# Attention and experts on one core: the pair's shared tile in two column groups, eight places for weights, other orders at passage and end

## The reference

```python
Q, K, V = ste_sign(x * sign(bv_q)), ste_sign(x * sign(bv_k)), x * sign(bv_v)
attn = where(causal, sigmoid(einsum('btd,bsd->bts', Q, K) * d**-0.5 * 4.0), 0.0)
x = layernorm(x + einsum('bts,bsd->btd', attn, V))
probs = softmax(x @ w_router); top1 = argmax(probs); gate = probs[top1]
pos = place of the token among those of its expert; accepted = pos < 320
g, u = rows @ w_gate[e], rows @ w_up[e]              # rows: accepted tokens of expert e
y = (silu(g) * u) @ w_down[e]                        # w_gate, w_up, w_down: 256 x 256
x = layernorm(x + where(accepted, y * gate, 0))
```

## Time and profile before

| | |
|---|---|
| median of 3 runs | 561.88 us (561.63 to 563.4) |
| the profiled execution | 564.1 us |
| its span, first to last instruction | 562.3 us |
| PE busy | 526.3 us (94%) |
| DVE busy | 409.3 us (73%) |
| ACT busy | 375.4 us (67%) |
| POOL busy | 371.1 us (66%) |
| mean granted clock of TensorE | 0.987 of full speed |
| moved by DMA | 81.53 MB |

### The profile page before, as it was taken

One profiled execution on the slowest core, in us unless ns is written; L12 is line 12 of the kernel. 1 busy time (PEld: TensorE's weight loads), 2 busy tenths in 40 slices (PEclk: granted clock), 3 DMA queues, 4 the chain that ended last, 5 costly groups with the idle time before them and its releaser, 6 DMA issues.

```text
span 562.3 us, 12210 instructions
## 1 busy us (share of the span) xinstructions
PE 526.3 (94%) x4024; PEld 475.7 (85%) x4062; DVE 409.3 (73%) x1029; ACT 375.4 (67%) x743; POOL 371.1 (66%) x496
## 2 busy tenths in 40 slices
PE   6999999999999999999999889999999999999970
PEld 5889898898978988888989359999989999998960
DVE  4785868867878857779586447888878887878860
ACT  5886968859677787677784215666666667667641
POOL 4647878687777768696772631676757667676672
PEclk9999999999999999999999999999999999999995
DMA  7994233243322532313910063676767677766410
GB/s 253 372 354 145 76 95 79 91 133 98 116 70 77 164 95 99 71 38 45 325 54 22 21 170 86 190 206 203 209 188 217 196 211 204 224 180 216 143 37 25
DMA packets 91902, 81.53 MB, mean 145 GB/s; under 512 B 31626, under 2 KB 83066, under 8 KB 91840
## 3 DMA queue, kind: packets, MB, share of 16 engines
q1 hardware_dynamic: 84848, 66.39, 40.6%
q0 software_dynamic: 6912, 14.30, 7.1%
q10 hardware_dynamic: 80, 0.07, 0.0%
HBM read 44.33 MB, written 37.90 MB: 146 GB/s over the span
## 4 chain that ended last, share of the span: by engine, by line
PE 69%; DVE 9%; issue 8%; DMA 5%; POOL 2%; ACT 2%; SPq 2%; another core or an unknown queue 1%; DVEq 0%; POOLq 0%; ACTq 0%
PE ps L884 11%; PE ps L885 10%; PE ps L886 10%; PE ps L860 9%; PE ps L1035 5%; PE ps L1043 4%; PE ps L1036 4%; PE ps L1061 4%; DMA xall<-in_L_ffn_w_down_dram 3%; PE ps L903 2%; PE ps L1013 2%; PE ps L1058 1%; DVE hl_ring L1127 1%; PE ps L916 1%; POOL out_dram L593 1%
## 5 line engine op out<-in xcount | busy, mean ns | idle before, releaser
L884 PE MATMUL ps<-v_hl,hl_ring 128*128 128x256 f32 x544 | 176.1, 324 | 0.5 <-DVE hl_ring L1127 0.3
L885 PE MATMUL ps<-v_hl,hl_ring 128*128 128x256 f32 x544 | 153.4, 282 | 0.0
L886 PE MATMUL ps<-v_hl,hl_ring 128*128 128x256 f32 x544 | 153.1, 281 | 0.0
L593 POOL DMA_INDIRECT out_dram<-alone,ids x80 | 97.0, 1213 | 37.6 <-issue 32.5
L884 PEld LDWEIGHTS ps<-v_hl,hl_ring 128*128 128x128 f32 x544 | 103.3, 190 | 15.7 <-issue 1.1
L1127 DVE TENSOR_TENSOR hl_ring<-ps,hl_ring 128x512 fp32r<-128x512 f32 (+3 forms) x160 | 93.2, 600 | 18.6 <-ACT ps L669 14.3
L885 PEld LDWEIGHTS ps<-v_hl,hl_ring 128*128 128x128 f32 x544 | 103.6, 190 | 2.4
L886 PEld LDWEIGHTS ps<-v_hl,hl_ring 128*128 128x128 f32 x544 | 103.2, 190 | 0.0
L667 ACT ACTIVATE hl_ring<-ps 128x512 fp32r<-128x512 f32 (+3 forms) x160 | 85.9, 537 | 25.2 <-PE ps L863 10.4
L669 ACT ACTIVATE ps<-ps 128x512 f32<-128x512 f32 (+3 forms) x160 | 87.0, 544 | 0.0
L1035 PE MATMUL ps<-hl_ring,v_hl 128*128 128x320 f32 x256 | 82.5, 334 | 2.0 <-DVE act_r L1341 1.5
(11 more groups left out here) (154 smaller groups left out, 1091.8 us busy)
## 6 DMA issues: line engine op xcount, KB each, us to landing
expert_rows<-xs SPq DMA_DIRECT2D x40, 258.0 KB, 5.3
xs<-expert_rows SPq DMA_DIRECT2D x32, 258.0 KB, 2.8
xall<-in_L_attn_x_dram SPq DMA_DIRECT2D x16, 512.0 KB, 4.8
out_dram<-alone SPq DMA_DIRECT2D x16, 512.0 KB
xall<-in_L_ffn_w_gate_dram SPq DMA_DIRECT2D x32, 256.0 KB
xall<-in_L_ffn_w_up_dram SPq DMA_DIRECT2D x32, 256.0 KB
xall<-in_L_ffn_w_down_dram SPq DMA_DIRECT2D x32, 256.0 KB
xs<-expert_rows SPq DMA_DIRECT2D x31, 64.5 KB
```

The source lines that it names most:

```text
L593: g_.indirect_dma_start(out=out_rows, out_offset=bass.IndirectOffsetOnAxis(ap=ids[:, e % NIDS, t:t + 1], axis=0), in_=o_s[:, p, t, :], in_ ...
L884: mm(o, ah, v_hl[:, 0, j, :], start=(j == 0 and i % 2 == 0), stop=False, skip_group_check=True)
L885: mm(o, ah, v_hl[:, 1, j, :], start=False, stop=False, skip_group_check=True)
L886: last = mm(o, al, v_hl[:, 0, j, :], start=False, stop=(j == GT * g + i), skip_group_check=True)
```

## The change

- `down` computes two tiles for each expert. For the shared tile an odd expert's `down` has four f32 matmuls in addition, without zeros: for each half of the hidden values one of the even expert into partitions 0 to 63 of bank 7 and one of the odd expert into partitions 64 to 127, with 64 stationary columns each. Their first half of the hidden values is a new f32 copy `act_q` of ACT, a second instruction in `high_hidden`, ahead of the old one; `act_r` keeps only 256 columns. The zeros' memsets at the start go.
- Raw weights have eight places (UR = 8). The first four experts' are issued before the last transposing DMA, the next four behind it; then two experts' (e+7 and e+8) are issued together after the `down` of each odd e.
- z, its statistics and the normalised rows have three buffers instead of two.
- Passage: for the last group the first two tiles' statistics come before the second residual; `place` and the second part of `gate` for the group before move behind the last statistics and behind the last normalisation. The last group's exponentials come from ACT's Exp, with one table load more. `high_x` of expert 0 is split between ACT and DVE, with two instead of four warming matmuls behind the first transposes.
- End: the last expert's second tile goes to bank 0, and `combine` takes its tiles one by one.

```diff
@@ -136,7 +136,8 @@
         slot = sb("slot", [P, 2, GT], U32)
 
 
-        raw = xall[:, 0:6 * U, :].rearrange("p (s k) f -> p s k f", k=6)
+        UR = 2 * U
+        raw = xall[:, 0:6 * UR, :].rearrange("p (s k) f -> p s k f", k=6)
 
...
         HN = FC * CAP
         act_s = a_buf[:, 0:HN].rearrange("p (k t) -> p k t", k=FC)
-        act_h = sb("act_h", [P, 2, CAP + CREST], F32)
-        act_r = sb("act_r", [P, 2, 2, CAP + CREST], F32R)
+        act_h = sb("act_h", [P, 2, CAP], F32)
+        act_r = sb("act_r", [P, 2, 2, CFULL * P], F32R)
+        act_q = sb("act_q", [P, U, CREST], F32)
         xs = sb("xs", [P, U, CT, ROW], F32)
...
+        def stored(e):
+
+            return 16 * sum(len(tiles_of(o)) for o in range(e % 3, e + 1, 3))
+
...
-        def pair_tile_cols(e, t):
-
-            if t == CFULL:
-                return (0, P) if e % 2 else (CFULL * P, CFULL * P + P)
-            lo = t * P + (e % 2) * P
-            return lo, lo + P
+        def sums(e, t):
+
+            if e == E - 1 and t == 1:
+                return ps[:, 0, 0:D]
+            return ps[:, 6 + t // 2, (t % 2) * D:(t % 2 + 1) * D]
+
+        def rest_cols(e):
+
+            return (0, CREST) if e % 2 else (CFULL * P, CAP)
 
         def own_cols(e):
 
-            return (e % 2) * CREST, (e % 2) * CREST + CAP
...
+            def load_raw(e):
+                for n, w in enumerate((w_gate, w_up, w_down)):
+                    sp.dma_start(raw[:, e % UR, 2 * n:2 * n + 2, :],
+                                 w[e].rearrange("(c p) f -> p c f", p=P)).then_inc(raw_in[e % UR], 16)
+
             turn_signs(B - 1, 2)
             store_alone((B - 1) * NG - 1, (NG - 1) % 2)
+            for e in range(U):
+                sp.wait_ge(res_ready, 6 * (e + 1))
+                load_raw(e)
             turn_signs(B - 1, 3)
-
-            def load_raw(e, s):
-                for n, w in enumerate((w_gate, w_up, w_down)):
-                    sp.dma_start(raw[:, s, 2 * n:2 * n + 2, :],
-                                 w[e].rearrange("(c p) f -> p c f", p=P)).then_inc(raw_in[s], 16)
 
...
-                sp.wait_ge(wh_ready, e + 1)
-                sp.wait_ge(wl_ready, e + 1)
-                sp.wait_ge(y_done, (e + 1) * CT)
-                load_raw(e + U, e % U)
-                atleast(sp, os_out[e % 2], 16 * (CFULL + e % 2) * (e // 2 - 1))
+                if e % 2 and e + UR < E:
+                    sp.wait_ge(wh_ready, e + 1)
+                    sp.wait_ge(wl_ready, e + 1)
+                    sp.wait_ge(y_done, tiles_to(e + 1))
+                    load_raw(e + UR - 1)
+                    load_raw(e + UR)
+                if e >= U:
+                    sp.wait_ge(os_out[(e - U) % 3], stored(e - U))
                 load_ids(e + U)
...
+            act.wait_ge(table_ready, 1)
+            s_.activation(spare[:, :], spare[:, :], ACT.Exp).then_inc(table_ready, 1)
             normalise(B * NG - 1, 2 * B - 1, 1, range(GT // 2))
             copy_x1t(B * NG - 1, range(1))
             copy_lgt(B * NG - 1)
-            gates(B * NG - 1)
-            act.wait_ge(table_ready, 1)
+            act.wait_ge(below_ready, B * NG)
+            act.wait_ge(gate_ready, B * NG - 1)
+            s_.activation(quot[:, :, :], below[:, :, :], ACT.Exp).then_inc(exp_ready, 1)
+            act.wait_ge(table_ready, 2)
             s_.activation(spare[:, :], spare[:, :], ACT.Silu).then_inc(table_ready, 1)
...
+                atleast(act, y_done, tiles_to(e - 1) if e > 1 else 0)
+                s_.activation(act_q[:, e % U, :], ps[:, 3, slice(*rest_cols(e))], ACT.Copy).then_inc(hr_ready, 1)
+                s_.activation(act_r[:, p, 0, :], ps[:, 3, lo:hi], ACT.Copy).then_inc(hh_ready, 1)
 
             def second_norm(R, n):
                 e, p = R * U + n, n % 2
                 act.wait_ge(zrs_ready, e + 1)
...
-            high_x(0, 0)
+            act.wait_ge(xs_turned, 1)
+            s_.activation(x_h[:, 0, 0, 0:CT * P], ps[:, 0, 0:CT * P], ACT.Copy).then_inc(xh_ready, 1)
...
-                e, s, p = R * U + n, n % U, n % 2
+                e, s, p = R * U + n, (R * U + n) % UR, n % 2
                 pe.wait_ge(hl_ready, e + 1)
                 pe.wait_ge(h_ready, e + 1)
-                pe.wait_ge(raw_in[s], 48 * (R + n // U + 1))
+                pe.wait_ge(raw_in[s], 48 * (e // UR + 1))
                 atleast(pe, z_step, tiles_to(e))
                 wh, wl = w_h[:, e % 3, 4, :], w_l[:, e % 3, 4, :]
-                for t in range(CT):
-                    bank, side = 6 + t // 2, slice((t % 2) * D, (t % 2 + 1) * D)
-                    lo, hi = pair_tile_cols(e, t)
-                    o = ps[:, bank, side]
-                    mm(o, act_r[:, p, 0, lo:hi], wh, start=(t < CFULL or p == 0), stop=False, skip_group_check=True)
-                    mm(o, act_r[:, p, 0, lo:hi], wl, start=False, stop=False, skip_group_check=True)
-                    mm(o, act_r[:, p, 1, lo:hi], wh, start=False, stop=False, skip_group_check=True)
-                    last = mm(o, act_h[:, p, lo:hi], raw[:, s, 5, :], start=False, stop=True, skip_group_check=True)
+                lo, hi = own_cols(e)
+                for t in range(CFULL):
+                    o = sums(e, t)
+                    at, ah = slice(t * P, t * P + P), slice(lo + t * P, lo + t * P + P)
+                    mm(o, act_r[:, p, 0, at], wh, start=(t == 0 or e == E - 1), stop=False, skip_group_check=True)
+                    mm(o, act_r[:, p, 0, at], wl, start=False, stop=False, skip_group_check=True)
+                    mm(o, act_r[:, p, 1, at], wh, start=False, stop=False, skip_group_check=True)
+                    last = mm(o, act_h[:, p, ah], raw[:, s, 5, :], start=False, stop=True, skip_group_check=True)
+                    last.then_inc(y_done, 1)
+                if p == 1:
+                    pe.wait_ge(hr_ready, e + 1)
+                    for f in range(FC):
+                        for m in (e - 1, e):
+                            rows = slice((m % 2) * CREST, (m % 2) * CREST + CREST)
+                            h = act_q[:, m % U, :] if f == 0 else act_h[:, m % 2, slice(*rest_cols(m))]
+                            last = mm(ps[rows, 7, 0:D], h, raw[:, m % UR, 4 + f, :], start=(f == 0), stop=(f == FC - 1),
+                                      skip_group_check=True)
                     last.then_inc(y_done, 1)
...
-            keep_warm(4, bank=M0)
+            keep_warm(2, bank=M0)
...
@@ -1208,22 +1240,19 @@
             def place_and_gate(G, par):
 
                 base = G * SN + 4
-                dve.wait_ge(sg_ready, 2 * G + 2)
-                v_.reciprocal(quot[:, :, :], sg[:, 1, :, :]).then_inc(gate_step, 1)
                 dve.wait_ge(counts_done, G + 1)
                 v_.tensor_tensor(pm[:, :, :], hot[:, G % 2, 0:GT, :], logits, ALU.mult).then_inc(pos_read, 1)
-                dve.wait_ge(gate_step, 3 * G + 1)
-                v_.scalar_tensor_tensor(out=quot[:, :, :], in0=quot[:, :, :], scalar=2.0, in1=sg[:, 0, :, :],
-                                        op0=ALU.mult, op1=ALU.mult).then_inc(gate_step, 1)
+                dve.wait_ge(exp_ready, 1)
+                v_.tensor_reduce(rt[:, 1, :], quot[:, :, :], AX_X, ALU.add).then_inc(gate_step, 1)
                 dve.wait_ge(pos_read, G + 1)
                 v_.tensor_reduce(own_pos, pm[:, :, :], AX_X, ALU.add).then_inc(route_step, 1)
-                dve.wait_ge(gate_step, 3 * G + 2)
-                v_.tensor_reduce(rt[:, 1, :], quot[:, :, :], AX_X, ALU.add).then_inc(gate_step, 1)
+                dve.wait_ge(gate_step, 3 * G + 1)
+                v_.tensor_scalar(rt[:, 1, :], rt[:, 1, :], 2.0, None, ALU.mult).then_inc(gate_step, 1)
                 dve.wait_ge(route_step, base + 1)
                 v_.tensor_scalar(over, own_pos, CAP + 0.5, SKIP, ALU.is_gt, ALU.mult).then_inc(route_step, 1)
                 v_.scalar_tensor_tensor(out=rt[:, 0, :], in0=topd[:, :], scalar=-float(CAP), in1=own_pos,
                                         op0=ALU.mult, op1=ALU.add).then_inc(route_step, 1)
-                dve.wait_ge(gate_step, 3 * G + 3)
+                dve.wait_ge(gate_step, 3 * G + 2)
                 v_.reciprocal(xrow[:, par, :, D], rt[:, 1, :]).then_inc(gate_ready, 1)
...
-            add_pair(B - 1, 3, 0)
-            add_pair(B - 1, 3, 2)
+            residual(G, 0, B * NS - GT + 2, 1)
+            row_statistics(G, 0, 1)
+            residual(G, 2, B * NS, 1)
             statistics(G, 1)
+            place(G - 1, 0)
             dve.wait_ge(rstd_step, G * RN + 2 + 1)
             dve.wait_ge(scattered[1], (2 * B - 1) * 16 * GT)
             for i in range(GT // 2, GT):
                 v_.tensor_scalar(xrow[:, 1, i, 0:D], res[1][:, i, :], mv[:, i, 0:1], small[:, 1, i:i + 1],
                                  ALU.subtract, ALU.mult).then_inc(x1_late, 1)
+            gate(G - 1, 0, 1)
...
-                    atleast(dve, y_done, (e - 1) * CT)
-                    lo, hi = own_cols(e)
```

(45 more changed lines are left out.)

69 lines of the change are left out of this document (35 added, 34 removed).

## The result

The changed kernel takes 560.33 us (median; 559.91 to 560.36 over five runs). The kernel before, on the same chip in the same rounds, takes 562.61 (561.63 to 563.4). The ratio is 0.9959, with a 95% interval of 0.994 to 0.9979: 2.3 us or 0.4% faster, where the prediction said 5.7 us. 560.33 lies in the predicted range, 4.1 us above the predicted time. The predicted mechanism of turn A is there to a hundredth; one price and one subtraction were wrong.

The account below looks back on a forecast made before the run. PE was taken to bind odd experts' turns, DVE's chain even ones after the change, with late-weight stalls besides. Turns 3.25, passage 1.25 and end 1.23 sum to 5.73 us, from median 561.88 to 556.2; range 552 to 563.

Parts of the forecast that it names:

- The base: Starting time of the sum: the 5.73 us gain, worked out on an execution of 564.1, was subtracted from the median 561.88.
- Part 1, turn A: Even expert's down, one tile of 0.78 fewer: DVE's chain from the transposes delays gate_up, so 6.31 only becomes 6.16 us.
- R1: Rival: DVE's chain does not bind the even expert's turn; 0.63 us more saved in each of 15, 546.7; chance 0.07.
- Part 1, turn B: Odd expert's down: a tile of 0.78 becomes the shared tile of 1.03 in two column groups; 6.55 becomes 6.80 us.
- Part 2, stalls: Expert phase: eight weight places remove all stalls from late weights, 4.65 us over 28 turns; bounds 0 and 4.65.
- Net of parts 1 and 2: 28 expert turns: 4.65 us of stalls removed less 1.4 lost by the shared tile, a gain of 3.25 us.
- Part 3, passage: Attention to experts: earlier statistics 0.65, one Exp instead of two sigmoids 0.35, split high_x 0.25; together 1.25 us.
- Part 4, end: Last experts: last down a tile earlier 0.78, shared tile's z and statistic 0.45 earlier; together 1.23 us.
- The cap of 1.26: At the end, POOL's store at 547.49 lasts 0.97, the next can follow 0.30 later: at most 1.26 us gained.
- R4: Rival: eight weight places change nothing, as traffic and not lead makes loads late; 4.65 us back, 560.8; chance 0.14.
- R2: Rival: matmuls start strictly in order, so shared-tile halves overlap less; 0.21 more in 16 tiles, 3.4 us, 559.6; chance 0.13.
- R3: Rival: the shared tile's two halves do not overlap; 0.85 more in 16 tiles, 13.6 us, 569.8; chance 0.12.

Follow-up runs that it names:

- e2: The kernel before with eight places for raw weights and nothing else, loaded one expert at a time: 558.84 us, ratio 0.9944.
- e1: The kernel before, unchanged, profiled and timed once more: 562.46 us, ratio 1.0001.
- e4: The changed kernel with DVE's low_weights of the next expert moved to the head of its turn: 552.68 us, ratio 0.9836 to the kernel before.
- e6: The changed kernel with the shared tile's four matmuls issued twice in a row: 573.58 us.
- e5: The changed kernel with the shared tile's four matmuls issued group by group instead of alternating between groups: 560.12 us.
- e7: The changed kernel with four places for raw weights instead of eight: 673.12 us.

## Why the prediction was wrong, point by point

The miss is 560.36 (the profiled execution) against 556.2, 4.1 us. It has two parts.

**The base, 2.2 us.** The sum was made on an execution of 564.1 with a span of 562.3 and then taken from the median, 561.88. The step that failed is the sentence "the median of the three runs is 561.88, near the span". A time is the span and 1.8 us, before (564.1 - 562.3) and after (560.36 - 558.6). Predicted span 556.6 + 1.8 = 558.4 was what the prediction's own working gave for that execution. A sum that removes all stalls of one execution must start from the time of that execution: from 564.1 to the 559.38 of e2's profiled execution it is 4.7 us, as priced, but between medians (561.93 to 558.84) it is 3.1. Why the profiled execution stood 2.2 above the median is known in part: beside the one of e1 (562.99) its stalls are 0.3 longer and its way to the first `down` matmul 0.8.

**The span, 2.0 us.** 562.3 became 558.6, a gain of 3.7 instead of 5.73. Term by term:

- **Part 1, turn A:** predicted 6.16, measured 6.15. The chain, its 3.40, L1373's 0.42, the 0.15 to `gate_up`: all right, and e4 shows that this chain is what binds. R1 is refuted.
- **Part 1, turn B:** predicted 6.80, measured 6.97. This is the step that failed: the price of the tile, "0.85 + 0.18 = 1.03", taken from the router. The stream of 0.85 was right (e6). Entry and exit are 0.35. 14 x 0.17 = 2.4 us, and this is the whole shortfall of the span and 0.4 more. In the router only the gap before it was used as a price; its 0.14 over the ideal was called "16 small starts" and dropped for another 0.09. Had the prediction added the 0.09 and the 0.14, as the rows had them, the tile would have been 1.08, and 0.7 us of the 2.4 explained. The rest, an exit of 0.19 before an f32r matmul with weights of 128 columns, no row of before shows. The prediction's 0.09 for the way out was an estimate, set equal to the 0.09 in; no run shows it, and the runs show 0.10 in, 0.05 in the first step and 0.19 out.
- **Part 2, stalls:** predicted 4.65 of the profiled execution. After has no ACT wait for w_down, and its turns are all at their bound, so the term was right for that execution; e2 measures it alone at 4.6 us in the turns of the profiled executions and 3.1 us between medians.
- **Net of parts 1 and 2:** predicted 3.25, measured 184.69 - 183.63 = 1.06. Of the difference of 2.2, 2.4 is the tile.
- **Part 3, passage:** predicted 1.25, measured 339.94 - 338.57 = 1.37. POOL's first step at 310.50 is 0.63 earlier than the same step of before, at 311.13 (predicted 0.65). That closeness is in part luck. Profiles with the same passage differ here by more than the miss: POOL's step is at 310.63 to 311.30 in the three with the old passage and at 309.80 to 310.78 in the seven with the new one; the first `down` matmul is at 339.17 to 339.94 and at 338.01 to 338.96. The means of the latter differ by 1.2.

```profile
310.50 0.22 POOL L497 TENSOR_SCALAR small<-mv 128x4 f32<-128x4 f32 x1 [11.70 <-DVE mv L1181]
...
318.96 0.29 DVE L1244 TENSOR_TENSOR pm<-hot,ps 128x128 f32<-128x128 bf16 x1 [0.48 <-PE ps L960]
...
331.19 0.49 ACT L840 ACTIVATE hl_ring<-ps 128x384 fp32r<-128x384 f32 x1 [12.17 <-PE ps L1044]
331.19 0.56 DVE L1418 CAST hl_ring<-ps 128x384 fp32r<-128x384 f32 x1 [0.62 <-PE ps L1044]
```

  `pm` starts 0.85 earlier than in the earlier trace rows, of which 0.63 came with POOL's step; the exponentials gave 0.22 and not 0.35, as pm now waits for PE's counts (0.48 idle). high_x halves as predicted (0.56 instead of 0.81). These make 1.10; the other 0.27, of which 0.20 lies between pm and high_x, the prediction did not have.
- **Part 4, end:** predicted 1.23, measured 37.67 - 36.40 = 1.27. z of the shared tile starts 2.88 after the last down (predicted 2.9). The cap of 1.26 took POOL's earlier stores as fixed. Counted from the 29th down the store at 544.85 comes 0.2 earlier than its match of before (547.49), and the one behind it waits 0.49 for ACT where 0.30 is the usual gap, so two small errors that cancel give the cap's number:

```profile
539.34 0.36 PE L1086 MATMUL ps<-v_hl,act_r 128*128 128x256 f32 x1 [1.10 <-issue]
...
542.22 0.48 DVE L1392 SCALAR_TENSOR_TENSOR z<-ps,xs 128x256 f32<-128x256 f32 x1
...
544.85 0.97 POOL L611 DMA_INDIRECT out_dram<-alone,ids  x1 [0.30 <-issue]
546.31 0.97 POOL L611 DMA_INDIRECT out_dram<-alone,ids  x1 [0.49 <-ACT alone L825]
...
548.87 0.98 POOL L611 DMA_INDIRECT out_dram<-alone,ids  x1 [0.30 <-issue]
```

- **R4** (560.8) and **R2** (559.6) are the numbers nearest to the result, both for reasons that do not hold. R4 is refuted by e2. For R2 the order of issue changes nothing (e5); its agreement was a coincidence of 0.21 and 0.17. **R3** (569.8) is refuted by the 1.02 us for eight passes.

With both parts corrected the sum is 556.2 + 2.2 + 2.4 - 0.3 (passage, end, turn A at 6.15, which came out better) = 560.5, against 560.36.

The prediction said that a tile price of 1.39 would make the whole change worth nothing. It did not ask the question next to it: at which price does the shared tile itself lose, with turn A bound by DVE? A pair saves 0.15 in A, so the tile must cost under 0.78 + 0.15 = 0.93 in B. Neither 1.03 nor 1.20 does. By the prediction's own numbers the shared tile lost time in the turns (1.4 us) and was paid for at the end alone; the experiments show that moving one step of DVE's order turns it into a gain of 4.6 us.

## What to carry to other kernels

Before an engine's work is cut, look for the chain that will hold that engine instead, and move the step of the chain that hangs on something else (here the weights, which depend neither on the transposes nor on down): the cut is worth its length only then. Price a passage into column groups and out of them as a sum paid once per visit (here 0.35 us, with eight matmuls as with four), and put as much as possible into one visit. And subtract a sum that was made on one execution from that execution's time, not from a median of others; a term of some tenths of a microsecond is known only as well as executions of one kernel agree in it.

## What the hardware did that I had not expected

- The order of issue did not matter between two column groups of the array, in the two orders tried: with the even expert's two f32 matmuls issued ahead of the odd one's, all eight passes and the way to `gate_up` still took 1.02 us, as when alternating (e5).
- Going into two column groups and out of them costs 0.35 us at this place: 0.10 in, 0.05 in the first step, 0.19 out.
- PE's signal that half of `gate_up` is done came 0.85 to 1.10 us after the modelled end of its matmuls in 6 turns of one kernel (e4), and ACT's `silu` began by as much late; the cause is open.
- The granted clock was 0.75 as the mean of a turn in which PE was busy for 7.27 us of 13.84 (e7), 0.50 from 444 to 449 us with PE idle until 447.00, and 1.00 in the next turn; behind the wait matmuls started 0.27 apart and not 0.15.
